# Criss-cross attention with two channel tiles per pass, an accumulator for each, and the residual loaded into the accumulators

## What is computed

```python
def _L0_conv_ref(x, Wq, bq, Wk, bk, Wv, bv, gamma):
...
    q = jnp.einsum('bchw,oc->bohw', x, Wq) + bq[None, :, None, None]
    k = jnp.einsum('bchw,oc->bohw', x, Wk) + bk[None, :, None, None]
    v = jnp.einsum('bchw,oc->bohw', x, Wv) + bv[None, :, None, None]
    eH = jnp.einsum('bchw,bcpw->bhwp', q, k)
    eH = jnp.where(diag, -jnp.inf, eH)
    eW = jnp.einsum('bchw,bchp->bhwp', q, k)
    att = jax.nn.softmax(jnp.concatenate([eH, eW], axis=3), axis=3)
    attH, attW = (att[..., :H], att[..., H:])
    outH = jnp.einsum('bcpw,bhwp->bchw', v, attH)
    outW = jnp.einsum('bchp,bhwp->bchw', v, attW)
    return gamma.reshape(()) * (outH + outW) + x
```

## Time and profile before

| | |
|---|---|
| median of 3 runs | 4829.86 us (4828.94 to 4844.14) |
| the profiled execution | 4835.99 us, of which the span from first to last instruction is 4834.2 us |
| PE busy | 75% of the span |
| DVE, ACT, POOL busy | 48%, 41%, 25% |
| mean granted TensorE clock | 0.863 of 2.4 GHz |
| moved by DMA | 1180.34 MB, mean 244 GB/s |

### The profile page before, as it was taken

How to read it: one execution, slowest core, us unless ns; L and a number is a source line. 1 busy time by engine, 2 the same in 40 slices (tenths; PEclk the granted TensorE clock), 3 DMA queues, 4 the chain that set the end, 5 groups by cost and what they waited for, 6 DMA issues and landing times.

```text
span 4834.2 us, 92235 instructions
## 1 busy us (share of the span) xinstructions
PE 3601.8 (75%) x32472; PEld 2369.9 (49%) x32472; DVE 2321.5 (48%) x3322; ACT 1975.2 (41%) x3852; POOL 1220.7 (25%) x979
## 2 busy tenths in 40 slices
PE   4978778587885878858777587766887678874765
PEld 2435555355552555526554265543655445553655
DVE  6648443484334743357433564436543275433522
ACT  2425534154442544325443354333543245342632
POOL 0000342204321042311423014320143202431233
PEclk9989998798997989979898798987998889987656
DMA  7876699956998669986799867997599975999299
GB/s 281 288 226 218 180 280 292 276 188 192 296 282 272 189 186 301 294 257 197 198 291 288 249 195 213 299 274 253 167 252 299 260 254 160 268 305 239 76 263 270
DMA packets 995049, 1180.34 MB, mean 244 GB/s; under 512 B 48896, under 2 KB 788224, under 8 KB 988416
## 3 DMA queue, kind: packets, MB, share of 16 engines
q1 hardware_dynamic: 939264, 1023.06, 75.3%
q10 hardware_dynamic: 55296, 151.02, 8.5%
HBM read 834.15 MB, written 339.74 MB: 243 GB/s over the span
## 4 chain that ended last, share of the span: by engine, by line
issue 53%; PE 11%; DMA 10%; POOL 10%; SPq 9%; ACT 3%; DVE 2%; ACTq 0%; POOLq 0%; DVEq 0%
DMA xr<-x 6%; POOL e_grp L489 6%; SPq L387 5%; POOL xr L499 3%; DMA v_in<-v_pixel_major 3%; SPq L377 3%; PE banks L955 3%; PE banks L957 2%; PE banks L956 2%; POOL qk_lo L471 1%; SPq L323 1%; ACT acc L609 1%; PE banks L1027 1%; PE banks L1029 1%; PE banks L1028 1%
## 5 line engine op out<-in xcount | busy, mean ns | idle before, releaser
L955 PE MATMUL banks<-wv_hi,x_hi 128*128 128x512 f16 x2304 | 961.6, 417 | 401.0 <-DVE v_out L758 264.5
L758 DVE SCALAR_TENSOR_TENSOR v_out<-banks,proj,v_out 128x512 f16<-128x512 f32 x576 | 431.8, 750 | 1525.6 <-ACT v_out L560 1523.2
L499 POOL TENSOR_TENSOR xr<-xr,acc 128x768 f32<-128x768 f32 x384 | 721.7, 1888 | 1074.4 <-DVE acc L825 636.3
L956 PE MATMUL banks<-wv_lo,x_hi 128*128 128x512 f16 x2304 | 951.8, 413 | 0.0
L957 PE MATMUL banks<-wv_hi,x_lo 128*128 128x512 f16 x2304 | 945.3, 410 | 0.0
L609 ACT ACTIVATE acc<-banks,gbv_col,att 128x384 f32<-128x384 f32 x768 | 694.7, 996 | 302.7 <-POOL xr L499 183.3
L560 ACT ACTIVATE v_out<-banks,proj 128x512 f16<-128x512 f32 x576 | 390.6, 682 | 935.4 <-PE banks L957 757.6
L471 POOL TENSOR_TENSOR qk_lo<-qk_f,qk_hi 128x384 f16<-128x384 f32 x192 | 178.0, 927 | 2114.2 <-ACT qk_hi L568 2106.7
L1027 PE MATMUL banks<-prob_col,v_in 96*128 96x96 f16 x3072 | 479.1, 217 | 239.5 <-ACT acc L609 118.1
L1027 PE MATMUL banks<-prob_row,v_in 96*128 96x96 f16 x3072 | 472.1, 217 | 140.7 <-DVE acc L825 79.1
L955 PEld LDWEIGHTS banks<-wv_hi,x_hi 128*128 128x128 f16 x2304 | 244.0, 106 | 675.5 <-DVE v_out L758 276.7
(11 more groups left out here) (99 smaller groups left out, 6455.6 us busy)
## 6 DMA issues: line engine op xcount, KB each, us to landing
v_in<-v_pixel_major SPq DMA_DIRECT2D x768, 384.0 KB, 8.7
x_raw<-x SPq DMA_DIRECT2D x195, 768.0 KB, 6.5
v_pixel_major<-v_out SPq DMA_DIRECT2D x576, 256.0 KB, 4.7
x_next<-x SPq DMA_DIRECT2D x192, 768.0 KB, 6.1
xr<-x SPq DMA_DIRECT2D x384, 384.0 KB, 10.3
out<-xr ACTq DMA_DIRECT2D x384, 384.0 KB, 6.4
x_first<-x SPq DMA_DIRECT2D x24, 768.0 KB, 8.0
qk_halves<-qk_hi SPq DMA_DIRECT2D x192, 96.0 KB, 2.1
```

Of the source, the lines that this page charges most:

```text
L499: nc.gpsimd.tensor_tensor(xr[u][:, :], xr[u][:, :], acc[:, c * CPX:(c + 1) * CPX], ALU.add).then_inc(res_added, 1)
L758: nc.vector.scalar_tensor_tensor(out=v_out[tile % V_OUT][:, :, 1, :], in0=bank[tile % 2][:, :].rearrange("p (t c) -> p t c", t=CT), scalar ...
L955: nc.tensor.matmul(dst, s_hi, m_hi, start=(t == 0), stop=False)
L956: nc.tensor.matmul(dst, s_hi, m_lo, start=False, stop=False)
```

## The change

- **Two channel tiles at a time.** `TT` = 2, `TP` = 2: groups alternate between two channel tiles on the same four strips (`group_at`), each tile with its own accumulator `acc0`, `acc1`. A `v_in` load keeps its 384 KB, now four strips of two channel tiles, so a contiguous piece is 1 KB. `GROUPS` stays 192, in two halves (`HALF` = 96). The probabilities of a strip group are prepared once per two groups of the first half.
- **The residual is loaded into the accumulators.** Both kinds of groups are added to `acc` on DVE (`add_group`); `evacuate_column`, `add_residual` on POOL and the `xr` buffers are gone. Every chunk gets the bias on ACT, in place, and is stored from the accumulator (`store_chunk`). For the first pair of tiles `acc0` is loaded with one transfer of whole rows and `acc1` with two; for the second pair a chunk is reloaded when its store has landed (`reload_residual`). A column group needs its whole accumulator loaded.
- **Items.** `BLK` = 256: a block is two value items and one q-and-k item, 108 items per image. Head 18, pairs 12 (one with every second pair), statistics 14, attention 64: 27 beside the first half, 10 between the halves (`TURN`), 27 beside the second.
- **Memory.** The second accumulator takes the place of `xr`, `e_grp`, a second `qk_f32`, a fourth `v_out` and larger blocks. `x_next` has two buffers instead of four and lies, as does low k, in the memory of `acc1`; the scan of the maximum therefore starts behind `load_qk` (item 6) and ends in the statistics. Probabilities are normalised in place.
- **Scores.** Low k is loaded once, on 64 partitions, and multiplied with high q alone (`qs[0:CQ]`); the product of the two low halves falls away.
- **SP.** An item stores the values of the item before it. `load_qk` comes after item 6 instead of before item 0 and waits for all output stores first; the first six `v_in` loads come right behind it.

```diff
-    BLK = 4 * W
+    BLK = 256
...
-    VS = 2 * G
+    TT = 2
+    TP = CT // TT
+    HALF = 2 * NG * TT
+    GROUPS = TP * HALF
...
-    NXT = 4
+    NXT = 2
...
-    V_OUT = 4
+    V_OUT = 3
...
-    HEAD = 8
-    STATS = 5
-    S_ITEMS = HEAD + PAIRS + STATS
+    QK_AT = 6
+    HEAD = 18
+    HEAD_SCAN = HEAD - QK_AT - 2
+    STATS = 14
+    TURN = 10
+    S_ITEMS = HEAD + PAIRS // 2 + STATS
...
         def group_at(i):
-            return i // (2 * NG), (COL, ROW)[i // NG % 2], i % NG
+            return i // HALF, (COL, ROW)[i // (NG * TT) % 2], i // TT % NG, i % TT
...
             def load_qk(b):
                 for s in range(2):
                     wait_alone(sp, qk_stored[s], (b + 1) * (ROUNDS["x"] * 32) + 32)
-                wait_alone(sp, res_added, b * CHUNKS + ONE0)
-                halves = [slice(c * HW // 2, (c + 1) * HW // 2) for c in range(2)]
-                for c, px in enumerate(halves):
+                for tt in range(TT):
+                    for c in range(NCH):
+                        wait_alone(sp, out_stored[tt][c], b * (TP * 16) + 16)
...
+            def reload_residual(b, tt, c):
+                sp.wait_ge(out_stored[tt][c], b * (TP * 16) + 16 + 16)
+                px = slice(c * CH, (c + 1) * CH)
+                sp.dma_start(acc[tt][:, px], x_acc[b, TT + tt, :, px]).then_inc(acc_loaded[tt], 16)
...
                 wait_alone(sp, s_ready, (b + 1) * PAIRS)
-                for i in range(XR):
-                    load_residual(b, i)
+                sp.dma_start(acc[0][:, :], x_acc[b, 0, :, :]).then_inc(acc_loaded[0], 16)
+                sp.dma_start(acc[1][:, 0:HW // 2], x_acc[b, 1, :, 0:HW // 2]).then_inc(acc_loaded[1], 16)
                 for k in range(STATS):
                     if items:
-                        item(b + 1, HEAD + PAIRS + k)
+                        item(b + 1, HEAD + PAIRS // 2 + k)
+                    if k == 5:
+                        wait_alone(sp, factor_row_ready, b + 1)
+                        if items:
+                            wait_alone(sp, xmax_own_ready, b + 3)
+                        sp.dma_start(acc[1][:, HW // 2:HW], x_acc[b, 1, :, HW // 2:HW]).then_inc(acc_loaded[1], 16)
...
-            def evacuate_column(b, g):
-                t, o, h = group_at(g)
-                if h == 0:
-                    act.wait_ge(res_added, (b * CT + t) * NCH + ONE0)
-                act.wait_ge(o_mm, b * GROUPS + g + 1 + ONE0)
-                nc.scalar.activation(
-                    acc_strips[COL][:, h * G:(h + 1) * G, :], out_bank[g % OUTS], ACT.Identity,
-                    scale=att[:, O_FACTOR:O_FACTOR + 1], bias=gbv_col[:, t:t + 1],
-                ).then_inc(col_evac, 1)
...
+            def store_chunk(b, g):
+                tp, o, h, tt = group_at(g)
+                px = slice(h // 2 * CH, (h // 2 + 1) * CH)
+                act.wait_ge(acc_added, b * GROUPS + g + 1 + ADDED0)
+                nc.scalar.activation(
+                    acc[tt][:, px], acc[tt][:, px], ACT.Identity, bias=gbv_col[:, tp * TT + tt:tp * TT + tt + 1]
+                ).then_inc(bias_added, 1)
...
-            def add_row(b, g):
-                t, o, h = group_at(g)
-                if h == 0:
-                    dve.wait_ge(col_evac, (b * CT + t + 1) * NG + ONE0)
+            def add_group(b, g):
+                tp, o, h, tt = group_at(g)
+                if h == 0 and o == COL:
+                    done = FIRST_LOADS[tt] * 16 if tp == 0 else RESIDUALS[tt]
+                    wait_alone(dve, acc_loaded[tt], b * RESIDUALS[tt] + done)
+                if h == 0 and o == ROW and tt == 0:
+                    wait_alone(dve, acc_added, b * GROUPS + g + ADDED0)
                 dve.wait_ge(o_mm, b * GROUPS + g + 1 + ONE0)
-                a = acc_strips[ROW][:, h * G:(h + 1) * G, :]
+                a = acc_strips[tt][o][:, h * G:(h + 1) * G, :]
                 nc.vector.scalar_tensor_tensor(
                     out=a, in0=out_bank[g % OUTS], scalar=att[:, O_FACTOR:O_FACTOR + 1], in1=a,
                     op0=ALU.mult, op1=ALU.add,
...
-                        last = nc.tensor.matmul(dst[:, g, :], qs, kl, start=False, stop=(o == ROW))
+                        last = nc.tensor.matmul(dst[:, g, :], qs[0:CQ], kl, start=False, stop=(o == ROW))
```

More of the change, by code:

```diff
@@ L437, in _ @@
             batch(B - 1, False)
[L438 to L439 removed]
+            for tt in range(TT):
+                for c in range(NCH):
+                    sp.wait_ge(out_stored[tt][c], B * (TP * 16) + 16)
         @block.gpsimd
```

447 lines of the change are left out of this document (229 added, 218 removed).

## The result

The changed kernel takes 5129.62 us (median of 4 runs, 5118.41 to 5143.25), the kernel before beside it 4834.62 us (4828.94 to 4844.14). The ratio is 1.0609 with a 95% interval of 1.0575 to 1.0644: 6.1% slower. The forecast was 4616 us, faster. The profiled execution spans 5141.4 us at a mean granted clock of 0.826, before 0.863.

A forecast was written before the change was run, and what follows sets the result against it. Limits differ by stage: DVE bounds the attention columns, transfers the first half's rows. Head 89, pairs 103, statistics 34 and attention 332 make 558 us per image for 586.4; with last image and prologue the median forecast is 4616, range 4390 to 4840.

The forecast's parts named there:

- head: Start of an image, now with 18 items for 8: 89 us for 61, with PE standing still some 20 us.
- pairs: Score stage of 24 pairs, half an item beside each: 4.3 us per pair, 103 us for 129; dropped low product brings 0.
- statistics: Stage before attention with 14 items for 5: PE 30 us, accumulator loads and landing 32, together 34 us for 22.
- columns, first half: Column groups of the first channel tile pair: DVE-bound at 1.09 us per column addition, 84 us.
- rows, first half: Row groups of the first channel tile pair: 94 us of DMA with 24 stores and 18 reloads, a few sliding away: 90 us.
- gap: Ten items between the attention halves: PE 21.5 us, covering the last store and six reloads; 22 us.
- columns, second half: Column groups of the second channel tile pair: DVE 67, PE 53, DMA 49 us; 69 us.
- rows, second half: Row groups of the second channel tile pair: DMA 67 us, last stores spilling into the next image's start; 63 us.
- turn: Passage to the next image: the wait for POOL and its last chunk is gone, 4 us.
- Rival two: Column additions on DVE cost 1.57 us, bound the columns and make the kernel slower, 4991 us; decides from about 1.38; chance 0.13.
- The value load: Load of 0.393 MB in 1024 B pieces: falls from 1.74 to 1.33 us, at an estimated 296 GB/s.
- rival three: Longer pieces bring nothing: value loads stay at 1.74 us, 20 us per image, kernel 4768 us; chance 0.06.

The follow-up runs named there:

- klo128: The changed kernel with low k loaded on both partition halves again and multiplied with both halves of q (128 rows): 4715.71 us, ratio 0.9762 to before.
- before_klo64: The kernel before with only the product of the two low halves left out (low k times high q on 64 rows): 5349.63 us, ratio 1.1072.
- klo128_v512: klo128 with each value load issued as two transfers of one channel tile each, in pieces of 512 B: 4720.39 us, ratio 0.9759.
- klo128_noreload: klo128 without reloading the residual for the second pair of channel tiles, whose outputs are then wrong: 4517.28 us, ratio 0.9335.

## Why the prediction was wrong

The sum for a steady image was 558 us; 630.4 came. Point by point (klo128 is the kernel after without the alternation):

| stage | forecast | after | klo128 |
|---|---|---|---|
| head | 89 | 88 | 94.5 |
| pairs | 103 | 158 | 101 |
| statistics | 34 | 46 | 46.5 |
| columns, first half | 84 | 80 | 79 |
| rows, first half | 90 | 79 | 75.5 |
| gap | 22 | 44 | 42.5 |
| columns, second half | 69 | 61 | 61 |
| rows, second half | 63 | 64 | 65.5 |
| turn | 4 | 10 | 10.2 |

- **The step that failed** is the last sentence on the pairs: "Matmul count and columns of the scores stay, whatever the rows, so the dropped low product brings 0." Count and columns did stay. But the two matmuls of a product now have different row counts, and at each step from one to the other the weight load no longer runs beside the matmul before. That costs PE 0.13 us on rows and 0.20 to 0.24 on columns: the pairs took 158 us for 103, which is 55 of the 72 us missed per image. klo128 gives 414 us of the kernel back and before_klo64 makes the loss alone, 514 us. I had priced the smaller matmul and not the change from one kind to the other, and none of the rivals was about PE. No row of before that I looked at had 64 rows and 128 in turn, so the term had no source and needed bounds; it got 0. PE, 84 us of 101 in the pairs of klo128, had room for only some of the 65 us of steps; the rest came out as time.
- **The other slower case came true only in its sign.** Rival two needed a column addition above 1.38 us. It took 42.35 us of DVE for 46 additions in the first column quarter, 0.92 us each, for 1.09 taken; the rows took 28.98 for 49, 0.59. So a strided read and write side by side cost DVE 0.33 more, less than ACT's 0.48 for the write alone. This is why the column stages came out 4 to 8 us below forecast. The rule on lines of 16 bytes ("Advanced Engine Details and Errata", Memory Cachelines, in the Trainium skill) excluded 0.61, and the trace agrees.

```profile
1237.00:1317.00 80.00, 42.35 (x46) 0.94 0.65 183
1317.00:1396.00 79.00, 28.98 (x49) 0.95 1.01 320
```

These two rows are the addition line alone (DVE busy us and its count, clock, DMA share, GB/s).

- **The value load was mis-sized.** I took 1.33 us for 384 KB; 239 GB/s make it 1.64, and klo128_v512 shows no gain at all: what rival three said, longer pieces bring nothing, is what happened, and I had given it 0.06. Rows of the first half and gap together were forecast at 112 us and took 123 (118 in klo128). They differ from the forecast more in where the time lies: I let 18 of 24 reloads run within the rows and six in the gap. In the image shown of after only 12 landed before the gap and 12 in it, where the items' transfers run too. klo128_noreload shows what the reloads cost, 22 us in a steady image, for 25 priced.
- **The statistics** were forecast at 34 us from the accumulators and five items' transfers. In klo128 46.5 us at 315 GB/s are 14.6 MB: 9.4 MB of accumulators, as I had counted (7.1 and then 2.4), and 5.2 MB of items. I had counted PE for 14 items and DMA for five. Nine items more at the 1.28 us of the prediction are 12 us, which is what is missing in each image.
- **Head and turn.** 88 us for 89, with the stall of PE (28 us in one piece, for some 20 forecast). The turn takes 10 us for 4: POOL's wait is gone, but in the kernel after PE still waits 8 us there for an item's `x_lo` of DVE, which waits 5.8 us for ACT.
- **Without the failed step** the forecast would still have been low by 100 us (4716 against 4616): 12.5 in the statistics, 6 in rows and gap, 5.5 in the head, 6 in the turn and 2.5 in the last rows, less 13 in the columns and 2 in the pairs, are 17.5 per image (575.7 measured for 558, rounded), 122 for seven. The last image gave 32 back (4710.7 - 4343.3 = 367 us for 399). That lies within the 25 us per image that I gave the stages, and 4716 lies in the range. That it comes so near is partly luck: the columns' 13 us, from an addition of 0.92 us for 1.09, cancel the statistics' 12.5. So the sign and the range failed by one line of the diff.

## What to carry to other kernels

Price a matmul by what stands before it on TensorE too: where matmuls of 64 rows stand beside ones of 128 or 96, keep those with one count together, or pad the smaller and compute what isn't needed. Look at the weight loads in the trace: one that starts only with its own matmul is the sign. Between 96 and 128 rows it did not appear here. When a diff has many edits, bound also the one that looks harmless: 360 steps per image of 0.13 to 0.24 us were worth more than the rest of the change. And count a stage's transfers for every item in it before its compute; a stretch at a DMA share of 1 moves its time elsewhere when its neighbours are changed.
